# A sparse graph layer on one core: two of the four loads of each tile of the second pass move from SyncE's DMA queue to ScalarE's

## The reference, cut to what matters

```
h = relu(layernorm(x))
e = leaky_relu(h @ a1 + (h @ a2).T)            # N x N
U = softmax(where(adj > 0, e, -inf), axis=1)
rowsum = sum(U * 0.5 * U, axis=1)
feat = soft_threshold(f(h, U @ h, rowsum))     # first product with U
out  = x + g(feat, U @ feat, h0, rowsum)       # second product with U
```

## Time and profile before

| | |
|---|---|
| median of 3 runs | 1499.63 us (1499.61 to 1502.81) |
| profiled execution | 1504.1 us, span 1502.5 us |
| second pass in the profile | from about 1069 us to 1499 us |
| POOL busy, whole span | 604.6 us (40%) |
| PE busy, whole span | 966.3 us (64%) |
| TensorE clock granted | 0.801 on average |

### The profile page before, as it was taken

How to read it: one execution, slowest core, us unless ns; L and a number is a source line. 1 busy time by engine, 2 the same in 40 slices (tenths; PEclk the granted TensorE clock), 3 DMA queues, 4 the chain that set the end, 5 groups by cost and what they waited for, 6 DMA issues and landing times.

```text
span 1502.5 us, 28009 instructions
## 1 busy us (share of the span) xinstructions
PE 966.3 (64%) x3629; PEld 575.2 (38%) x3630; DVE 931.8 (62%) x5233; ACT 864.4 (58%) x1840; POOL 604.6 (40%) x649
## 2 busy tenths in 40 slices
PE   3545677777776677667777776764465465545666
PEld 3521254444443343333333433332344244433333
DVE  7756557677778888888888888876311123333343
ACT  4673677877888888888888888851212121111111
POOL 1005354443432333222222222127566666656663
PEclk9975687888989988988887878775576777787887
DMA  6989887899999999999999999933434445556664
GB/s 182 362 288 361 332 316 291 321 339 350 363 350 376 369 359 381 374 385 374 372 382 378 378 375 373 382 105 88 128 100 129 116 141 153 142 165 173 184 188 142
DMA packets 152838, 415.71 MB, mean 277 GB/s; under 512 B 31694, under 2 KB 115678, under 8 KB 136406
## 3 DMA queue, kind: packets, MB, share of 16 engines
q1 hardware_dynamic: 122492, 345.66, 62.1%
q0 software_dynamic: 30304, 69.62, 15.2%
HBM read 398.37 MB, written 33.90 MB: 288 GB/s over the span
## 4 chain that ended last, share of the span: by engine, by line
DVE 30%; issue 27%; PE 13%; another core or an unknown queue 10%; ACT 5%; DMA 5%; SPq 4%; DVEq 3%; ACTq 2%; POOLq 0%; POOL 0%
PE ACC L689 3%; PE TP L321 3%; DVE XHO L1066 2%; PE ACC L693 2%; ACT SG L309 2%; PE MISC L987 2%; DMA R<-in_x_dram 1%; DVEq L257 1%; DVE RE L1198 1%; PE ACC L694 1%; SPq L1600 1%; SPq L1602 1%; SPq L1599 1%; SPq L1601 1%
## 5 line engine op out<-in xcount | busy, mean ns | idle before, releaser
L309 ACT ACTIVATE SG<-W,ABOVE 128x4096 bf16<-128x4096 f32 x126 | 467.2, 3708 | 72.9 <-DVE cnt L1049 40.3
L634 POOL DMA_INDIRECT R<-haug_d,IDS x230 | 231.4, 1006 | 592.0 <-issue 577.9
L321 PE MATMUL TP<-SG,FOLD 128*128 128x512 bf16 x1008 | 299.8, 439 | 0.0
L680 ACT ACTIVATE DG<-ident,WSR 128x128 f32<-128x128 f32 x230 | 76.5, 393 | 353.7 <-remote 190.1
L1753 DVE SCALAR_TENSOR_TENSOR R<-ACC,SELF,R 128x256 f32<-128x256 f32 x63 | 30.5, 484 | 301.8 <-remote 191.0
L634 POOL DMA_INDIRECT W<-feat_d,IDR x140 | 141.9, 1013 | 75.0 <-issue 74.4
L689 PE MATMUL ACC<-R,DG 128*128 128x256 f32 x446 | 165.9, 525 | 0.4 <-issue 0.3
L321 PEld LDWEIGHTS TP<-SG,FOLD 128*128 128x128 bf16 x1008 | 113.5, 121 | 112.0 <-issue 50.3
L688 PE MATMUL ACC<-XHO,ZB 128*128 128x256 bf16 x126 | 40.8, 324 | 179.1 <-ACTq L682 77.9
L689 PEld LDWEIGHTS ACC<-R,DG 128*128 128x128 f32 x446 | 106.1, 255 | 21.6 <-issue 3.2
L689 PE MATMUL ACC<-W,DG 128*128 128x256 f32 x274 | 96.3, 494 | 7.5 <-issue 7.1
(11 more groups left out here) (295 smaller groups left out, 2290.5 us busy)
## 6 DMA issues: line engine op xcount, KB each, us to landing
W<-in_adj_dram SPq DMA_DIRECT2D x128, 2048.0 KB, 13.4
haug_d<-R POOLq DMA_DIRECT2D x8, 1056.0 KB, 9.9
HTS<-haug_d SPq DMA_DIRECT2D x64, 132.0 KB
R<-in_x_dram SPq DMA_DIRECT2D x8, 1024.0 KB, 6.6
R<-in_x_dram SPq DMA_DIRECT2D x64, 128.0 KB
R<-in_L_gnn_h_dram SPq DMA_DIRECT2D x64, 128.0 KB
R<-feat_d SPq DMA_DIRECT2D x64, 128.0 KB
out_dram<-R SPq DMA_DIRECT2D x64, 128.0 KB, 2.0
```

The lines of the kernel that those rows point to most:

```text
L309: nc.scalar.activation(SG[:, u, half(h)], W2[:, u, half(h)], ACT.Sign, scale=2.0 ** 100, bias=ABOVE[:], accum_out=DEG[:, u, h:h + 1]).then ...
L321: nc.tensor.matmul(KP[u], FOLD[:, b], SG[:, u, b * FW:(b + 1) * FW], start=False, stop=False)
L634: pool.indirect_dma_start(out=g[:, k, 0:w], out_offset=None, in_=table, in_offset=bass.IndirectOffsetOnAxis(ap=ids[:, k:k + 1], axis=0), * ...
L680: nc.scalar.mul(DG[:, u, k], ident[:], weights[:, k:k + 1])
```

## The change

The loads of x and h0 of tile t are no longer begun by SyncE ahead of those of feat and `pt_d`. ScalarE begins them on its own DMA queue when it has made tile t's diagonals, behind a wait for `finish(t-4)` of its own. The semaphore and the counts that TensorE and VectorE wait for stay.

```diff
@@ second_sync
                 if live(0):
                     sp.wait_ge(out_made, t - 3 + RING)
-                    sp.dma_start(XR[:, v], x[bass.ds(t * P, P), :]).then_inc(t2_loaded[v], 16)
-                    sp.dma_start(H0R[:, v], h0[bass.ds(t * P, P), :]).then_inc(t2_loaded[v], 16)
                     sp.dma_start(FR[:, v], feat_d[bass.ds(t * P, P), :]).then_inc(t2_loaded[v], 16)
                     sp.dma_start(PTR[:, v], pt_d[0, :, bass.ds(t * P, P)]).then_inc(t2_loaded[v], 16)
@@ second_scalar
                 act.wait_ge(staged, t + 1)
                 act.wait_ge(prod2_ready, t - 1 + RING)
                 diagonals(act, t, v % 2, WSR[:, v], diag2_begun, diag2_ready)
+                act.wait_ge(out_made, t - 3 + RING)
+                act.dma_start(XR[:, v], x[bass.ds(t * P, P), :]).then_inc(t2_loaded[v], 16)
+                act.dma_start(H0R[:, v], h0[bass.ds(t * P, P), :]).then_inc(t2_loaded[v], 16)
```

## The result

| | before | after |
|---|---|---|
| median (4 runs each, same chip) | 1501.22 us (1499.61 to 1505.09) | 1519.56 us (1515.37 to 1524.85) |
| ratio | | 1.0116, 95% interval 1.0088 to 1.0144 |
| profiled execution, and span | see the table ahead | 1517.16 us, 1515.5 us |

The change makes the kernel 18.3 us slower. The forecast was 1493 us and faster.

A forecast was written before the change was run, and what follows sets the result against it. SyncE's queue of loads was taken to bound the late second pass. Late part -16 us, early part +8, start +1: -7 us from the median 1499.6, so 1493 us, range 1478 to 1520.

The forecast's parts named there:

- rival B: TensorE's first matmul waits for late x and h0 as ScalarE is held: slower, 1515 to 1525 us; chance 0.35.
- The strong form of B: ScalarE held in all its instructions, some 20 a turn: 7.4 us a turn, +84 us at full strength.
- the term of -16 us for the late part: Second pass after 1298 us: SyncE relieved, 38 turns fall from 5.21 to 4.8 us each, -16 us.
- The early part's +8: Second pass before 1298 us: some eight bursts after held stretches step by the new loop and lose time, +8 us.
- the start's +1: Second pass's first tiles: their loads start about 1 us later, behind the first diagonals, +1 us.
- The loop: ScalarE's diagonals and loads, landing, TensorE's product: 7.9 us for two tiles unheld, 4.0 us a turn.
- The 1.5 us that I added for holding: ScalarE's two DMAs held 0.54 us each plus 0.4 us elsewhere: two tiles take 9.4 us, 4.7 a turn.
- GpSimd's floor of 4.4 us: Late second pass: GpSimd's gathers at their least gap are the next limit, 4.4 us a turn, -34 us.
- The price of a DMA on SyncE: SyncE's late turn: 0.54 us of holding for each of five DMAs; two fewer save 1.9 us.
- The holding of ScalarE: Whether ScalarE is held once it begins DMAs: no row shows it; DMA medians of 0.3 to 0.4 us expected.
- Rival C: GpSimd and held stretches set the pace, SyncE drags along: no change, 1496 to 1504 us; chance 0.20.

The follow-up runs named there:

- e10: Changed kernel with x and h0 on a semaphore of their own, for which only VectorE's finish waits; set with held stretches: ratio to the kernel before 1.0021.
- e11: The change unedited against the kernel before, in a set with held stretches (before 1503.9 us): ratio 1.0086.
- e1: Changed kernel with x and h0 on a semaphore of their own, for which only finish waits; set without held stretches: ratio to the kernel before 0.9993.
- e5: The change unedited against the kernel before, without held stretches: 1419.3 us against 1389.8, ratio 1.0209.
- e4: Kernel before with SyncE beginning all four loads, but x and h0 only after the tile's diagonals; without held stretches: ratio 1.0086.
- e14: Kernel before without the second pass's loads of x and h0, those terms missing from the output; ratio 0.9894.
- e15: Kernel before with the loads of x and h0 each cut into halves, so SyncE begins six loads, not four; ratio 1.0312.
- e13: Changed kernel with x and h0 on their own semaphore and begun ahead of the product wait and diagonals; with held stretches: ratio to the kernel before 1.0025.
- e2: Kernel before, all loads on SyncE, feat and pt_d first, x and h0 last on their own semaphore; without held stretches: ratio 1.0003.
- e3: Changed kernel with ScalarE's two loads ahead of the product wait and diagonals, semaphore shared; without held stretches: ratio to the kernel before 1.0006.
- e6: The kernel before, unedited, run again for its trace without held stretches: 1386.8 us, no ratio.

## Why the prediction was wrong

**The wait of rival B is what decided, without the holding that B gave as its cause.** TensorE's wait at the first matmul is ended by h0, from 1298 us on (41.6 us) and earlier (47.3), as B placed it. That this wait is the loss is shown by e10 against e11 and by e1 against e5, where it alone is taken away; e4 has lateness without ScalarE and loses 12 of 29.5 us. But B reckoned with a ScalarE that is held, and e5, with no holding at all, loses more than the change does with it. The strong form of B (a ScalarE turn of 7.4 us) did not come in the change. That the time, 1519.6, lies within B's 1515 to 1525 is therefore in part luck.

**The step that failed is the term of -16 us for the late part, 38 x (5.21 - 4.8).** Turns 25 to 63 took 5.6 us more, not 16 less. The profiled execution took 20.1 us more than forecast for it (1517.2 for 1497.1): this term missed by 21.6 us and the early ones by 1.5 the other way. The medians are 26.6 us apart (1519.6 for 1493); what is left of that is spread between executions. The early part's +8 and the start's +1 came to +7.5 us, all of it in turns 1 to 25 and none at the start. That size may be luck: no run tested the bursts that it was reckoned from. Four things in the late term were off:

- *The loop.* I put it at 7.9 us for two tiles without holding. Its medians in the change sum to 9.96 us for tiles 49 to 63. Of the 2.1 us between, 1.1 is TensorE from its first matmul to the product's end, which I read from one quick turn (3.4 us; median 4.5), 0.8 is the landing (1.9; median 2.7), and the rest is drain and wait, 0.47 for 0.3. The 1.5 us that I added for holding hid most of this: the pass goes at 4.82 us a turn without any holding (e5), what I forecast with it, and turns 49 to 63 of the change took 5.04.
- *Unlike turns.* I compared that loop, summed for a tile with two slots, with 5.21 us, the average of all turns after 1298 us. In the trace of before eleven of the tiles 25 to 63 have three slots, and turns 49 to 63, which have two, took 4.75 us, not 5.21. Against those a loop of 4.8 us gains nothing. In turns 25 to 49 the kernel before took 5.43 us a turn and the changed one 5.50, where I had put 4.8 for it; 17 of the 20 us by which turns 25 to 63 missed 38 x 4.8 lie there.
- *What the loop replaces.* I set its average against SyncE's. But SyncE may begin loads up to two tiles ahead, so a held stretch of one queue can be covered by buffers; the loop is tied to the product of t-2 and has no such cover. This is argued from the order of the waits and not tested. What e5 shows is that the loop makes loads late that never were: 68.4 us of TensorE's waits for h0 without any holding.
- *The ceiling.* GpSimd's floor of 4.4 us took its least gap for every gather. e14 shows that leaving the loads out altogether gives 16 us, the very sum that I forecast for moving them, and that GpSimd's queue is held too.

**The price of a DMA on SyncE.** 0.54 us of holding each, so 1.9 us for two, was too high: e15 has 0.95 for two. It split all of the turn's holding among five DMAs, though register moves, waits and branches are held as well.

**The holding of ScalarE**, the open point of the forecast: in the change its DMA instructions have medians of 340 and 394 ns, as foreseen. Its held time hardly grew (last section), so it isn't what made the change slow. But where the late wait is taken away (e10, e13), ScalarE's queue fills 37% and 30% of the chain, held instructions for a good part. It looks as if what SyncE was spared, ScalarE pays; that this is why e10 and e13 gain nothing is argued from the chains, and no run took ScalarE's holding away alone. e1, in a set without any holding (0.9993), shows no cost of those DMAs.

**Rival C** holds only where there are no held stretches: there GpSimd is the pace and two DMAs fewer are worth nothing (e1, e2, e3 within 0.1%).

Of the Trainium skill, the rule in "DMA: Bandwidth & Descriptors", "Issuing engines are not separate DMA queues", that a second queue saves only the begin time, would have given a small gain at most. The runs bear out that there is little to gain (e10 and e13, which take two DMAs off SyncE without the late wait, are no faster than before), but the rule doesn't bear on a load that becomes late, and on a held queue the begin time is not small (0.47 us for each added DMA in e15). The lock that the Trainium skill names in "Perfetto Trace Analysis", "DMA Instruction — HWDGE (DVE, Sync)", isn't seen: in e5's timeline SPq L1600 and ACTq L1646 run side by side from 1389.0, at 0.33 and 0.36 us. Over the whole second pass of e5 `pt_d`'s instruction was begun 20 times while one of ScalarE's DMAs was under way, with a median of 333 ns, and 21 times alone, with the same median.

No version with its whole output beat the kernel before. e2, with loads in SyncE's order and an own semaphore, equals it where it was measured.

## What to carry to other kernels

Before a load is moved behind other work, list every engine that waits on its semaphore, also those that don't read it. A load that one consumer needs at the end and another only counts at the start gets a semaphore of its own, and here that was worth 10 of the 13 us lost (e11 to e10). A loop that a move creates is to be summed from the medians of many turns, not from one quick one, and compared with turns of the same kind of tile, held gaps included. Leave the work out once (e14), and the ceiling is known before anything is moved.

## What the runs showed of the hardware

- The same kernel takes 1389.5 to 1389.8 us in two sets of runs and 1501 to 1514 us in the others, both on one chip (1389.8 and 1513.6 us). In the slower ones queue instructions of SP, ACT, POOL and PE start some 0.70 us after the one before, for stretches of several us and more, as in the chain of e10; in e6 POOL's gap is never above 0.3 us. Some 60 of the 110 us lie in the first pass: the first `finish` is at 1046.0 us in e6 and 1106.9 in the kernel before. What starts or ends this isn't known.
- The holding isn't tied to one queue. Counted in the traces as the time in queue instructions that start 0.69 to 0.74 us (or two or three times that) after the one before, from 1075 us on, SP has 277 us before, 90 after and 153 in e10; ACT has 72, 87 and 250; POOL 182, 77 and 155. In e1 to e6 none of the three is above 19 us. In the changed kernel, where queues wait for one another, less is held than before.
- Two loads of 128 KB land 1.8 to 3.9 us after the end of the second one's instruction, median 2.8 (e5); with held stretches the median is 2.0 to 2.3 (e11 and the change), and for the same two loads begun by SyncE 2.3 (e4). The spread within one trace is larger than any difference between these, and the burst of four in the earlier trace rows, 2.8 us, lies inside it, so nothing about bytes can be read from it.
- Two sequencers begin DMAs at the same time without lengthening each other's instructions much: in e5 `pt_d`'s takes 333 ns with or without one of ScalarE's under way.
